# Cross attention's probabilities turned in 32x32 blocks by VectorE and moved over HBM

## The reference

```
Q = x @ Wq.T + bq;  K_new = x @ Wk.T + bk;  V_new = x @ Wv.T + bv
K = past keys (7680 rows of the context), then K_new;  V likewise with V_new
scores = Q @ K.T / sqrt(1024) + mask              # 512 x 8192
out = softmax(scores) @ V                         # 512 x 1024
```

## Time and profile before

| | |
|---|---|
| median of 3 runs | 1421.27 us (1420.23 to 1421.32) |
| span of the profiled execution | 1418.8 us |
| TensorE busy | 1398.2 us (99%), 6676 matmuls |
| VectorE busy | 848.8 us (60%) |
| ScalarE busy | 530.4 us (37%) |
| POOL busy | 195.0 us (14%) |
| moved by DMA | 212.0 MB, mean 149 GB/s |
| projections | 0 to about 153 us |
| cross attention loop | about 153 to 888 us |

### The profile page before, as it was taken

One profiled execution on the slowest core, in us unless ns is written; L12 is line 12 of the kernel. 1 busy time (PEld: TensorE's weight loads), 2 busy tenths in 40 slices (PEclk: granted clock), 3 DMA queues, 4 the chain that ended last, 5 costly groups with the idle time before them and its releaser, 6 DMA issues. The chain is left out here.

```text
span 1418.8 us, 18184 instructions
## 1 busy us (share of the span) xinstructions
PE 1398.2 (99%) x6676; PEld 1146.5 (81%) x6676; DVE 848.8 (60%) x1234; ACT 530.4 (37%) x947; POOL 195.0 (14%) x276
## 2 busy tenths in 40 slices
PE   7999999999999999999999999999999999999999
PEld 6878888888888888888888888877777888888887
DVE  6665455555555555555555557586776776677665
ACT  3333232222322222223322222465532435676561
POOL 3000100000000000000000000163432013112023
PEclk9999999999999999999999999999999999999999
DMA  7466653333333333333333332200430456997766
GB/s 245 158 210 239 236 182 120 129 112 112 117 111 111 111 121 126 115 111 118 111 111 111 112 125 76 89 1 1 156 117 1 151 181 211 320 310 285 270 237 217
DMA packets 44638, 212.03 MB, mean 149 GB/s; under 512 B 5360, under 2 KB 5424, under 8 KB 32112
## 3 DMA queue, kind: packets, MB, share of 16 engines
q1 hardware_dynamic: 28720, 145.24, 29.7%
q0 software_dynamic: 11296, 48.94, 10.4%
q10 hardware_dynamic: 4560, 17.04, 3.0%
HBM read 186.55 MB, written 24.64 MB: 149 GB/s over the span
## 5 line engine op out<-in xcount | busy, mean ns | idle before, releaser
L32 PE MATMUL banks<-V_hi,b_PT_hi 128*128 128x512 f32 x512 | 205.6, 401 | 0.0
L1101 ACT ACTIVATE b_PT_hi<-banks 128x512 fp32r<-128x512 f32 x64 | 38.4, 599 | 446.1 <-PE banks L814 446.1
L34 PE MATMUL banks<-V_hi,b_PT_lo 128*128 128x512 f32 x512 | 200.2, 391 | 0.0
L33 PE MATMUL banks<-V_lo,b_PT_hi 128*128 128x512 f32 x512 | 199.6, 390 | 0.0
L34 PE MATMUL banks<-K_hi,QT_lo 128*128 128x512 f32 x512 | 199.4, 389 | 0.0
L32 PE MATMUL banks<-K_hi,QT_hi 128*128 128x512 f32 x512 | 199.3, 389 | 0.0
L33 PE MATMUL banks<-K_lo,QT_hi 128*128 128x512 f32 x512 | 199.2, 389 | 0.0
L1322 DVE TENSOR_TENSOR b_scores<-banks,b_scores 128x512 f32<-128x512 f32 x64 | 44.2, 691 | 198.8 <-PE banks L34 198.8
L681 POOL DMA_DIRECT2D b_scores<-mask x60 | 32.2, 537 | 638.5 <-PE banks L814 626.4
L2267 DVE TENSOR_TENSOR e_lo<-e_raw,e_hi 128x1024 fp32r<-128x1024 f32 x80 | 96.5, 1242 | 33.4 <-ACT e_hi L2094 32.5
L34 PEld LDWEIGHTS banks<-V_hi,b_PT_lo 128*128 128x128 f32 x512 | 96.1, 188 | 21.0
(11 more groups left out here) (334 smaller groups left out, 2737.1 us busy)
## 6 DMA issues: line engine op xcount, KB each, us to landing
raw<-kv SPq DMA_DIRECT2D x60, 1024.0 KB, 4.8
e_raw<-w_up SPq DMA_DIRECT2D x40, 512.0 KB, 5.4
e_raw<-w_down SPq DMA_DIRECT2D x40, 512.0 KB, 6.2
b_scores<-mask POOLq DMA_DIRECT2D x64, 256.0 KB, 2.9
d_s_raw<-shared_w SPq DMA_DIRECT2D x26, 512.0 KB, 4.5
raw<-xattn_w SPq DMA_DIRECT2D x11, 1024.0 KB, 6.8
y_dram<-c_zeros ACTq DMA_DIRECT2D x1, 6656.0 KB, 27.3
raw<-attn_w SPq DMA_DIRECT2D x6, 1024.0 KB, 4.7
```

The costliest lines, as they stand in the source:

```text
L32: pe.matmul(out, lhs_hi, rhs_hi, start=first, stop=False)
L33: pe.matmul(out, lhs_hi, rhs_lo, start=False, stop=False)
L34: return pe.matmul(out, lhs_lo, rhs_hi, start=False, stop=last)
L1101: act.activation(PT_hi[:, u % 2, :], T_ps[:, u % 2, :], ACT.Copy).then_inc(b["pt_hi"], 1)
```

## The change

Keys within a chunk are put in another order: token 128 j + 32 b + k goes to column 128 b + 32 j + k. The host lays out K and the mask that way, and the own keys are written in it by ScalarE and VectorE. For steps 0 to 62 TensorE no longer turns the probabilities. Instead VectorE turns the 16 x 4 blocks of 32x32 of the 128x512 tile where they stand (`turn_blocks`), SP stores the tile to `pt_dram` in HBM, waits for the landing, and loads it in four parts, one for each 32 partitions, into `p_in`; each part has rows of 512 bytes. `pt_hi` and `pt_lo` read `p_in` in place of PSUM, in runs of 32 elements, and write the order that `values` wants. Step 63 keeps its transposes on TensorE. SP's list of a step becomes: store, four loads, then the load of K or V. `s_sb` has two buffers in place of four, and `p_in` takes the place of the other two. `turned` lies where the zeros lay; the zeros are made and stored earlier, in group 3 of the projections, and `turn_blocks` of the first two steps waits for the end of that store.

```diff
+def score_order(x):
+    return x.rearrange("p (j b k) -> p b j k", j=4, b=4)
...
+        zeros = at("a_zeros", [P, D], F32, "lr")
...
+        def in_score_order(x, o):
+            return score_order(x) if o >= 16 else x
+        def as_tokens(x, o):
+            return x.rearrange("p (b j k) -> p b j k", b=4, j=4) if o >= 16 else x
...
+            pool.memset(zeros[:, :], 0.0).then_inc(consts_done, 1)
...
+                if g == 3:
+                    act.wait_ge(consts_done, 3)
+                    act.dma_start(y_dram[MINC * P:, :].rearrange("(c p) d -> p c d", p=P),
+                                  zeros[:, :].unsqueeze(1).to_broadcast([P, MAXC - MINC, D])
+                                  ).then_inc(y_cleared, 16)
                 for o in range(4 * g, 4 * g + 4):
                     act.wait_ge(biased, o + 1)
-                    act.activation(out_tile(o, True), tmp[:, o % 2, :], ACT.Copy).then_inc(out_hi, 1)
+                    act.activation(in_score_order(out_tile(o, True), o), as_tokens(tmp[:, o % 2, :], o),
+                                   ACT.Copy).then_inc(out_hi, 1)
...
-        zeros = at("c_zeros", [P, D], F32, "lr")
+        turned = at("b_turned", [P, 2, W], F32, "lr")
+        p_in = at("b_p_in", [P, 2, W], F32, "s_sb", 4096)
...
+        def by_query_groups(x):
+            return x.rearrange("p (i b q) -> p b i q", i=4, b=4)
+        def by_key_blocks(x):
+            return x.rearrange("p (b i q) -> p b i q", b=4, i=4)
...
-            def load(base, u):
-                sp.wait_ge(b["kv_split"], base + (u - 1))
-                sp.dma_start(raw[:, u % 2, :], ins["kv"][base + u]).then_inc(kv_loaded[u % 2], 16)
-            with sp.Fori(1, SPLITS // 2) as it:
+            def store_turned(base, u):
+                sp.wait_ge(b["turned"], base + (u + 1))
+                sp.dma_start(pt_dram[u % 2], turned[:, u % 2, :]).then_inc(b["pt_stored"], 16)
+            def load_turned(base, u, known):
+                sp.wait_ge(b["pt_stored"], base * 16 + 16 * (u + 1))
+                sp.sem_inc(d["waited"], 1)
+                if known >= 2:
+                    sp.wait_ge(b["pt_lo"], base + (u - 1))
+                for j in range(4):
+                    rows = slice(32 * j, 32 * j + 32)
+                    sp.dma_start(p_in[rows, u % 2, :].rearrange("p (i r) -> p i r", i=4),
+                                 pt_dram[u % 2].rearrange("(i k) (j r) -> j k i r", i=4, j=4)[j]
+                                 ).then_inc(b[f"pt_loaded{u % 2}"], 16)
+            def load_kv(base, u):
+                sp.wait_ge(b["kv_split"], base + (u + 1))
+                sp.sem_inc(d["waited"], 1)
+                sp.dma_start(raw[:, u % 2, :], ins["kv"][base + (u + 2)]).then_inc(kv_loaded[u % 2], 16)
+            def turn_probs(base, u, known):
+                store_turned(base, u)
+                load_turned(base, u, known)
+            for u in range(2):
+                turn_probs(0, u, u)
+                load_kv(0, u)
+            with sp.Fori(1, SPLITS // 2 - 1) as it:
                 for u in range(2):
-                    load(it * 2, u)
+                    turn_probs(it * 2, u, 2)
+                    load_kv(it * 2, u)
...
+            def load_rows(i):
+                sp.wait_ge(s["w_split"], i + 1)
+                sp.dma_start(raw[:, i, :].rearrange("p (t d) -> p t d", d=D),
+                             ins["x"][2 * i:2 * i + 2].rearrange("t p d -> p t d")).then_inc(kv_loaded[i], 16)
+            turn_probs(0, SPLITS - 2, SPLITS - 2)
+            turn_probs(0, SPLITS - 1, SPLITS - 1)
             sp.wait_ge(b["kv_split"], SPLITS)
             load_weights(0)
             load_weights(1)
-            for i in range(2):
-                sp.wait_ge(s["w_split"], i + 1)
-                sp.dma_start(raw[:, i, :].rearrange("p (t d) -> p t d", d=D),
-                             ins["x"][2 * i:2 * i + 2].rearrange("t p d -> p t d")).then_inc(kv_loaded[i], 16)
+            turn_probs(0, SPLITS, SPLITS)
+            load_rows(0)
+            turn_probs(0, SPLITS + 1, SPLITS + 1)
+            load_rows(1)
+            turn_probs(0, SPLITS + 2, SPLITS + 2)
...
-            for u in range(4):
-                pool.wait_ge(own_split, 8 if u < 2 else 21 + u)
-                pool.dma_start(s_sb[:, u, :], ins["mask"][u]).then_inc(mask_loaded[u], 16)
-            pool.memset(zeros[:, :], 0.0).then_inc(b["zeros_done"], 1)
+            def load_mask(base, u):
+                pool.wait_ge(b["turned"], base + (u - 1))
+                pool.dma_start(s_sb[:, u % 2, :], ins["mask"][base + u]).then_inc(mask_loaded[u % 2], 16)
+            for u in range(2):
+                pool.wait_ge(own_split, 8)
+                pool.dma_start(s_sb[:, u, :], ins["mask"][u]).then_inc(mask_loaded[u % 2], 16)
...
+            load_mask(0, 2)
+            load_mask(0, 3)
             with pool.Fori(1, STEPS // 4) as it:
                 for u in range(4):
-                    pool.wait_ge(b["pt_ready"], it * 4 + (u - 3))
-                    pool.dma_start(s_sb[:, u, :], ins["mask"][it * 4 + u]).then_inc(mask_loaded[u], 16)
-            pool.wait_ge(s["consts_done"], 3)
+                    load_mask(it * 4, u)
...
-            def transpose(base, u, known):
-                pe.wait_ge(b["exp_done"], base + (u + 1))
-                if known >= 2:
-                    pe.wait_ge(b["pt_lo"], base + (u - 1))
+            def transpose_last():
+                u = STEPS - 1
+                pe.wait_ge(b["exp_done"], STEPS)
                 for k in range(4):
-                    mm = pe.transpose(T_ps[:, u % 2, k * P:(k + 1) * P],
-                                      s_sb[:, u % 4, k * P:(k + 1) * P], ident[:, :])
+                    mm = pe.transpose(T_ps[:, u % 2, k * P:(k + 1) * P], p_in[:, u % 2, k * P:(k + 1) * P], ident[:, :])
                 mm.then_inc(b["pt_ready"], 1)
...
             def step(base, u, known):
                 scores(base, u, known)
-                if known >= 1:
-                    transpose(base, u - 1, known - 1)
                 if known >= 2:
                     values(base, u - 2, known - 2)
...
-                transpose(0, n - 1, n - 1)
+                transpose_last()
...
-            act.wait_ge(b["zeros_done"], 1)
-            act.dma_start(y_dram[MINC * P:, :].rearrange("(c p) d -> p c d", p=P),
-                          zeros[:, :].unsqueeze(1).to_broadcast([P, MAXC - MINC, D])
-                          ).then_inc(b["y_cleared"], 16)
             def pt_hi(base, u, known):
-                act.wait_ge(b["pt_ready"], base + (u + 1))
+                if known < STEPS - 1:
+                    act.wait_ge(b[f"pt_loaded{u % 2}"], base * 32 + 64 * (u // 2 + 1))
+                    out, probs = by_key_blocks(PT_hi[:, u % 2, :]), by_query_groups(p_in[:, u % 2, :])
+                else:
+                    act.wait_ge(b["pt_ready"], 1)
+                    out, probs = PT_hi[:, u % 2, :], T_ps[:, u % 2, :]
                 if known >= 2:
                     act.wait_ge(b["pv_ready"], base + (u - 1))
-                act.activation(PT_hi[:, u % 2, :], T_ps[:, u % 2, :], ACT.Copy).then_inc(b["pt_hi"], 1)
+                act.activation(out, probs, ACT.Copy).then_inc(b["pt_hi"], 1)
...
-                act.activation(s_sb[:, u % 4, :], s_sb[:, u % 4, :], ACT.Exp,
+                scores, probs = s_sb[:, u % 2, :], s_sb[:, u % 2, :]
+                if known == STEPS - 1:
+                    scores = scores.rearrange("p (j b k) -> p j b k", j=4, b=4)
+                    probs = p_in[:, u % 2, :].rearrange("p (b j k) -> p j b k", b=4, j=4)
+                act.activation(probs, scores, ACT.Exp,
...
-            def pt_lo(base, u):
+            def pt_lo(base, u, known):
                 dve.wait_ge(b["pt_hi"], base + (u + 1))
-                dve.tensor_tensor(PT_lo[:, u % 2, :], T_ps[:, u % 2, :], f32(PT_hi[:, u % 2, :]),
-                                  ALU.subtract).then_inc(b["pt_lo"], 1)
+                hi, lo, probs = f32(PT_hi[:, u % 2, :]), PT_lo[:, u % 2, :], T_ps[:, u % 2, :]
+                if known < STEPS - 1:
+                    hi, lo, probs = by_key_blocks(hi), by_key_blocks(lo), by_query_groups(p_in[:, u % 2, :])
+                dve.tensor_tensor(lo, probs, hi, ALU.subtract).then_inc(b["pt_lo"], 1)
+            def turn_blocks(base, u, known):
+                dve.wait_ge(b["exp_done"], base + (u + 1))
+                if known < 2:
+                    dve.wait_ge(y_cleared, 16)
+                else:
+                    dve.wait_ge(b["pt_stored"], base * 16 + 16 * (u - 1))
+                dve.transpose(turned[:, u % 2, :], s_sb[:, u % 2, :]).then_inc(b["turned"], 1)
...
-                    pt_lo(base, u - 1)
+                    pt_lo(base, u - 1, known - 1)
+                if known < STEPS - 1:
+                    turn_blocks(base, u, known)
...
+    pt_dram = nc.dram_tensor("pt_dram", (2, P, W), F32, kind="Internal").ap()
...
```

(36 more changed lines are left out.)

14 lines of the change are left out of this document (7 added, 7 removed).

## The result

The changed kernel takes 1395.87 us, median of 4 runs (1394.43 to 1397.71); the kernel before, on the same chip, 1420.75 us (1419.74 to 1421.32). The ratio is 0.9826, with a 95% interval of 0.9813 to 0.984: 1.7% faster. The forecast was 1398.9 us, the range 1389 to 1412.

What follows compares the result with a forecast made beforehand. The prediction took TensorE, never idle in the cross attention loop, as the bound: 1418.8 - 30.1 (transposes) + 7.2 (clearing) + 0.5 (loop start) = 1396.4 us of span, 2.5 above it for the median: 1398.9 us, range 1389 to 1412.

Steps and rivals of the forecast that it cites:

- The transposes, -30.1 us: Cross attention loop, TensorE: four transposes a step removed, 0.478 us in each of 63 steps, 30.1 us saved.
- The lower bound, 22.7: Smallest saving from the transposes: 63 x 0.36 us, if the longer spacing behind them has another reason.
- The turn on VectorE: `turn_blocks` in each loop step: 0.69 us taken, bounds 0.5 and 1.3 us.
- The round trip: Loop: store, wait and four loads of the turned probabilities, 5.5 to 6.3 us; 6.3 taken, hidden behind TensorE.
- The closed loop: ScalarE's `pt_hi`, next exponential, next turn and round trip: 8.7 us, to fit a 10.886 us step; 2.2 us left.
- threshold of 8.5 us: Round trip time from which the closed loop, not TensorE, was to set the step's pace.
- R: Time from the end of VectorE's turn to the landing of the last loaded part; 6.3 us taken.
- the rival: Round trip paces the loop at ScalarE's `pt_hi`: each us over 8.5 costs 63 us; 12 in 100.
- The start of the loop: TensorE's wait for the first turned probabilities near 170 us: 0.5 us, bounds 0 and 2.1.
- The clearing, +7.2 us: Projections, group 3: storing the zeros holds the last weight block's chain, so TensorE waits 7.2 us; bounds 0 and 10.6.
- a transfer and a half of 6.9: Clearing's middle case: between one chain transfer held 6.9 us (TensorE waits 3.7) and both (10.6).
- The offset: Median of the runs over the span of the profiled execution: 2.5 us added.

Runs made afterwards that it cites:

- experiment 3: The changed kernel with four identity transposes a step given back to TensorE, with no wait and no reader: 1428.0 us, ratio 1.0048 to the kernel before.
- experiment 4: The changed kernel with extra awaited stores of the turned tile in each round trip: one added 1398.67 us, two added 1505.6 us.
- experiment 2: The changed kernel with the clearing as eight transfers from a narrow zero tile, one in each of the loop's first eight steps: 1391.63 us.
- experiment 5: The changed kernel with VectorE splitting half 10's weights ahead of its wait for the last weight block, clearing still in group 3: 1398.08 us.
- the first kernel of experiment 2: The changed kernel with the clearing as eight transfers issued in a row by ScalarE at the start of the attention stage: 1409.43 us.
- late_clear: The changed kernel with the clearing moved behind the cross attention, eight transfers by SP from a narrow zero tile: 1390.16 us.

## Why the prediction was right, point by point

- **The transposes, -30.1 us.** Exact: 704.6 - 674.5 = 30.1. A period from 219.0 to 806.5 us is 587.5 / 54 = 10.880 us; 10.886 was forecast. The lower bound, 22.7, would have left out the longer spacing behind the transposes, which is theirs too (experiment 3).
- **The turn on VectorE.** 0.71 us for 0.69; the bounds 0.5 and 1.3 were not needed. The Trainium skill's figure ("VectorE: DVE Perf Modes", section "The three transpose paths") gave an estimated 1.24 us for four 128x128 bf16 blocks; one 128x512 float32 pass took 0.71, so the trace does not agree with that estimate.
- **ScalarE.** `pt_hi` over 32-element runs takes 0.632 us in place of 0.60: costing it at nothing was sound.
- **The round trip.** 5.5 us in the step shown, 5.6 in the median; I took 6.3, the upper of two sums. The mask load that starts 0.6 us after the store did not hold it: the store landed in 2.0 us (median; longest 4.3), the parts in 2.1 (longest 3.3). Against that, an issue of a part takes 0.43 us in SP's queue, not the 0.333 of the earlier trace rows, so the last goes out 1.3 us behind the first. The Trainium skill ("DMA: Bandwidth & Descriptors", section "Anatomy of one DMA") has about 2.0 us of fixed cost on a transfer issued by GpSimd, with the moving of the bytes on top. The parts' 2.1 us agree with that; the store's 2.0 us, moving included, are below it.
- **The closed loop.** The mechanism and its threshold of 8.5 us were right (8.6 by experiment 4). The slack of 2.2 us was worked out with R = 6.3; with the measured 5.5 the same sum gives 3.0, and 2.68 was found in the step shown, 2.9 in the median. What the rival had too dear is a disturbance of a few steps: R of 8.75 to 10.4 in six steps cost 3.6 us where its rule gives 5.6 (experiment 2).
- **The start of the loop.** Forecast 0.5 us, found 0: R of step 0 is 5.5. Step 1 has R = 7.8, because its store went out at 175.20 behind a key load issued at 171.68, and landed in 4.3 us. That the key load, moved behind the parts, can stand ahead of the next store when steps are short, I had not listed; the reserve covered it. The Trainium skill ("DMA: Bandwidth & Descriptors", section "Queues, rings and completion order") has a completion land behind the earlier writes of its engines; the 4.3 in place of 2.0 us agree with that.
- **The clearing, +7.2 us.** Mechanism and place right, size 5.4 (5.6 at the first mask addition): the block was 8.5 us late, where a transfer and a half of 6.9 gave 10.4. The store was held by 6.1 us, near the 6.9 worked out from the earlier trace rows, the load by only 2.4. The issue went out at 99.61, not at 101.4: a DMA of ScalarE's queue does not wait for the pass ahead of it. And TensorE's wait came as two gaps, 2.16 and 1.00 us with a stretch at the lower clock between them, not one of 7: the gap of half 10 and the clock were in no term of the sum.
- **The offset.** The median lies 2.0 us above the profiled span; 2.5 was added.

The errors all lie to one side: 7.7 us were forecast for the clearing and the start of the loop and 5.6 found (2.1), 0.4 came from behind the loop, 0.5 from the offset, 3.0 us in all. The best kernel of these runs is the change with the clearing one or two groups later: 1390.53 and 1389.73 us, below the kernel before by 30 us, which is the whole price of the transposes.

## What to carry to other kernels

When an engine that is never idle loses instructions, measure its spacing with and without them: slots lost times steps is the gain, and a latency put in their place costs nothing as long as two conditions hold, a pace (the closed loop that it forms must fit in a step) and a cover (the value must come before it is used); the pace decides in the long run, and a few late steps cost less than their excess. Look for the loss in what moves along with the change: here a store moved to a free-looking queue fell beside a chain with 3.2 us of room, and one group later it was free. An engine's DMA issues count as its work where large ones stand one right behind the other: eight held ScalarE for 19.8 us. A gap that moves to the place where an engine becomes the bound can cost more than its length, by the clock behind it (experiment 5).

## What the runs showed of the hardware

**A clock that dips after a short gap.** TensorE's granted clock in the stretch from 131 to 153 us of the changed kernel is 0.92. After the gap of 2.16 us it ran at full speed (2.4 GHz) for 1.5 us and then at the lower of its two levels, 1.2 GHz, from 135.62 to 139.03:

```profile
135.39 0.43 PE L39 MATMUL a_banks<-V_hi,K_lo 128*128 128x512 f32 x1
135.62 0.63 PE L37 MATMUL a_banks<-V_hi,K_hi 128*128 128x512 f32 x1
136.04 0.63 PE L38 MATMUL a_banks<-V_lo,K_hi 128*128 128x512 f32 x1
...
138.60 0.59 PE L38 MATMUL a_banks<-V_lo,K_hi 128*128 128x512 f32 x1
139.03 0.39 PE L39 MATMUL a_banks<-V_hi,K_lo 128*128 128x512 f32 x1
```

Eight spacings of 0.43 in place of 0.23 us are 1.6 us. They cost nothing in this kernel: in the one with the idle transposes the same stretch has a granted clock of 1.00, its two gaps come to 5.1 us in place of 3.2, and its loop starts at 164.4, here at 164.6. TensorE only waited the less. Where no second wait takes it up, the dip does cost: in experiment 5 the lower level behind the gap of 5.73 us delayed the loop by 1.4 us, and in the first kernel of experiment 2 some 2.3 us came on top of the gap of 16.4. What decides whether a gap of 2 to 3 us brings a dip stays open: behind 2.16 us there was one, behind 2.48 and 2.61 us none.

**Large transfers issued in a row hold the engine that issues them.** ScalarE's issue of the whole clearing from the wide tile (6656 KB, one DMA) took 0.44 us; eight issues of 832 KB in 512 B rows, one right behind the other, took 19.80 us (0.44 the first, 2.99 the median), and one a step 0.38 us each. SP's eight in `late_clear` took 2.67 us each (median), so it is not ScalarE's alone. No run shows what the issues wait for.

**The same 6.5 MB land in 24.0 to 32.7 us**: 32.7 at group 3, 32.6 at group 4, 27.3 at the loop's start, 24.0 at group 5. What else ran at the time differs, but that this is the reason was not tested.
